# Rotary attention: the fourth turned fill of a pair moves from behind the first half of the values' projection to behind the third projection

## The reference, cut to what matters

```python
def _L0_attn_b_ref(x, Wq, Wk, Wv, Wo, bo):
    q = split_heads(x @ Wq); k = split_heads(x @ Wk); v = split_heads(x @ Wv)
    q = apply_rope(q); k = apply_rope(k)
    sim = jnp.einsum('bid,bjd->bij', q, k) * scale
    sim = jnp.where(causal[None], sim, -jnp.inf)
    attn = jax.nn.softmax(sim, axis=-1)
    out = jnp.einsum('bij,bjd->bid', attn, v)
    out = out.reshape(b, h, t, d).transpose(0, 2, 1, 3).reshape(b, t, h * d)
    return out @ Wo + bo
```

## Time and profile before

| | |
|---|---|
| median of the runs shown | 4107.78 us (4107.56 to 4110.89, 3 runs) |
| the profiled execution: its time | 4110.04 us |
| its span (first to last instruction) | 4108.3 us |
| the attention that the change touches | from about 1253 to 2720 us of the span |
| granted TensorE clock over the span | 0.911 |

### The profile page before, as it was taken

How to read it: one execution, slowest core, us unless ns; L and a number is a source line. 1 busy time by engine, 2 the same in 40 slices (tenths; PEclk the granted TensorE clock), 3 DMA queues, 4 the chain that set the end, 5 groups by cost and what they waited for, 6 DMA issues and landing times. The chain is left out here.

```text
span 4108.3 us, 88859 instructions
## 1 busy us (share of the span) xinstructions
PE 3521.3 (86%) x30527; PEld 2152.3 (52%) x30527; DVE 2730.1 (66%) x7270; ACT 2282.9 (56%) x5504; POOL 2039.0 (50%) x2055
## 2 busy tenths in 40 slices
PE   5999999967676999999999999985947776887768
PEld 1333333316673555655555555564936665675446
DVE  6888888856354777777777777754556664655465
ACT  2776777754233666666666666642435552674367
POOL 3333333217445676777767767656521111665175
PEclk9999999985797999999999999975979887898879
DMA  5434334302462121211212121122632221120001
GB/s 98 62 58 59 59 59 59 59 5 79 146 191 63 47 52 44 52 47 48 51 44 52 46 49 48 46 63 81 210 98 69 61 66 45 29 63 6 1 1 42
DMA packets 418239, 252.21 MB, mean 61 GB/s; under 512 B 251186, under 2 KB 344354, under 8 KB 416642
## 3 DMA queue, kind: packets, MB, share of 16 engines
q1 hardware_dynamic: 409156, 228.56, 24.2%
q0 software_dynamic: 8640, 17.97, 1.3%
HBM read 75.12 MB, written 41.75 MB: 28 GB/s over the span
## 5 line engine op out<-in xcount | busy, mean ns | idle before, releaser
L2499 POOL TENSOR_TENSOR ra_prob<-ra_prob,ra_inverse 128x256 f32<-128x256 f32 (+3 forms) x512 | 630.7, 1253 | 386.9 <-DVE ra_inverse L2715 386.6
L2313 DVE TENSOR_REDUCE ca_mx<-ca_ps_s 128x2 f32<-128x1024 f32 x512 | 601.0, 1211 | 122.5 <-PE ca_ps_s L2177 122.3
L2242 ACT ACTIVATE ca_pT<-ca_ps_p 128x512 f32<-128x512 f32 x1024 | 548.6, 602 | 219.6 <-PE ca_ps_p L2187 217.8
L2644 ACT ACTIVATE ra_prob<-ra_ps_s,ra_low 128x128 f32<-128x128 f32 (+3 forms) x1024 | 533.6, 531 | 237.8 <-DVE ra_low L2695 237.8
L2695 DVE CUSTOM_DVE_ANT_0 ra_ps_s<-ra_ps_s,ra_mask 128x128 f32<-128x128 f32 (+3 forms) x1024 | 475.3, 516 | 46.6 <-PE ra_ps_s L2592 46.4
L2177 PE MATMUL ca_ps_s<-ca_kst,ca_qst 128*128 128x512 bf16 x1024 | 394.5, 391 | 36.9 <-DVE ca_mx L2313 21.7
L2187 PE MATMUL ca_ps_p<-ca_qst,ca_kst 128*128 128x512 bf16 x1024 | 386.2, 382 | 4.4 <-ACT ca_pT L2242 3.9
L2650 ACT COPY ra_probT<-ra_ps_t 128x512 f32<-128x512 f32 x384 | 227.1, 591 | 278.6 <-PE ra_ps_t L2538 278.6
L2538 PE MATMUL ra_ps_t<-ident,ra_prob 128*128 128x128 f32 x2560 | 377.4, 278 | 5.1 <-POOL ra_prob L2499 1.2
L2538 PEld LDWEIGHTS ra_ps_t<-ident,ra_prob 128*128 128x128 f32 x2560 | 289.3, 141 | 124.2 <-issue 59.7
L2592 PE MATMUL ra_ps_s<-ra_kz,ra_qz 64*128 64x128 f32 (+3 forms) x2048 | 347.7, 458 | 3.7 <-DMA ra_kz<-ra_rot 2.8
(11 more groups left out here) (410 smaller groups left out, 7156.0 us busy)
## 6 DMA issues: line engine op xcount, KB each, us to landing
moe_w_own<-moe_w1T SPq DMA_DIRECT2D x142, 256.0 KB
ra_qz<-ra_rot SPq DMA_DIRECT2D x512, 64.0 KB, 2.0
ra_kz<-ra_rot SPq DMA_DIRECT2D x512, 64.0 KB, 2.0
ca_kst<-ca_bounce SPq DMA_DIRECT2D x256, 64.0 KB
ca_bounce<-ca_thirds SPq DMA_DIRECT2D x192, 64.0 KB, 2.8
ca_qst<-ca_bounce SPq DMA_DIRECT2D x64, 192.0 KB
moe_hs<-moe_rows SPq DMA_DIRECT2D x142, 66.0 KB
moe_raw<-in_L_ffn_W SPq DMA_DIRECT2D x32, 256.0 KB
```

Of the source, the lines that this page charges most:

```text
L2242: nc.scalar.activation(pT[:, (NS * hp + u) % PRING, :], ps_p[n % NP][:], ACT.Exp).then_inc(sg["drained"], 1)
L2313: nc.vector.tensor_reduce(mx[:, hm % 2, 2 * j:2 * j + 2], ps_s[m % 2][:].rearrange("p (b k) -> p b k", b=2), AX.X, ALU.max)\
L2499: nc.gpsimd.tensor_tensor(at, at, inverse[:, n % PROB, 2 * tile:2 * tile + 2].unsqueeze(2).broadcast_to([P, 2, keys]), ALU.mult)\
L2644: nc.scalar.activation(prob[:, n % PROB, tile, head, 0:keys], part(n, tile)[:, head, :], ACT.Exp, bias=low[:, n % PROB, at:at + 1], scale= ...
```

## The change

In the table of the turns, `turn(3)` leaves slot t=1 and goes to slot t=2, ahead of `turn(4)`. On TensorE it then stands behind `project(2)` or `project_out`, and no longer directly behind `turn(2)`. On DVE `fill(3)` moves with it, from ahead of the inverse of t=1 to behind `multiply(2)` or the addition to X, and ahead of `minima(2)`. No instruction is added or taken away, and the bank, the engine and the waits of each turn and fill stay as they are.

```diff
--- before.py
+++ after.py
@@ -2420,7 +2420,7 @@
         COPIES = 8
         landed = lambda n: 16 * COPIES * (n // RING + 1)
         VISITS = 3
-        fills = lambda t: ((0, 1), (2, 3), (4,), ())[t]
+        fills = lambda t: ((0, 1), (2,), (3, 4), ())[t]
         COPIED = (3, 2)
@@ -2726,8 +2726,10 @@
                     if score is not None and t == 0:
                         minima(0, score)
-                    if value is not None and t < 2:
-                        fill(2 * t + 1, value)
+                    if value is not None and t == 0:
+                        fill(1, value)
+                    if value is not None and t == 2:
+                        fill(3, value)
                     if t == 1 and 0 <= s - SCORE - 1 < PAIRS:
                         invert(s - SCORE - 1, 1)
```

## The result

| | before | after |
|---|---|---|
| median, both measured together (6 runs each) | 4107.67 us | 4141.03 us |
| lowest to highest | 4104.42 to 4111.05 | 4134.55 to 4148.47 |
| profiled execution, time (span) | 4110.04 (4108.3) us | 4135.67 (4134.0) us |

The changed kernel is slower by a ratio of 1.0081, 95% interval 1.0067 to 1.0095: 33 us of loss, 28 to 39. The forecast was 4143.5 us.

What follows compares the result with a forecast made beforehand. TensorE's instruction list was taken to bound the kernel (99.7% busy). 123 pairs x (0.53 new stop - 0.24 old stop) = 35.7 us on 4107.8 gave 4143.5 us, 4137 to 4147, widened to 4132 to 4160 for 8 in 10.

Steps and rivals of the forecast that it cites:

- The old stop, 0.24 us a pair: TensorE at turn(3), whose load waits for DVE's fill(1): 0.18 us waiting plus 0.06 restart, removed by the change.
- The new wait of 0.42 us behind the copy to v: TensorE, through with turn(2), waits 0.42 us before project(2) or project_out until ACT has copied v out of ps_r.
- The restart of 0.10 us: A projection starting without weights loaded ahead takes 0.10 us longer: L2563 1.12 for 1.02, L2573 2.05 for 1.95.
- The lower bound of 0.06: Restart of the projection bounded at 0.06 us, the transposes' price, giving a loss of 0.24 us a pair.
- The sum: Over the attention, 123 x (0.53 - 0.24) = 35.7 us more; bounds 29.5 and 39.4.
- The count of 123 pairs: Pair steps affected: 124 with a projection of v, less the first odd step, where nothing stands between the turns.
- It hangs on TensorE: ACT's copy to v would not come earlier against TensorE: a 2.61 us chain from turn(0) over fill(0) and exponentials.
- rival 1: Exponentials on ACT ahead of the copy to v start earlier, shrinking the new wait: faster, 4078.3 us; 7 in 100.
- fill(3) at no cost: On DVE, fill(3) pushes minima(2) by 0.32 us at most, covered by ACT's idle 0.73 and 1.88 us: cost nothing.
- rival 3: fill(3) ahead of minima(2) on DVE delays exponentials, fill(0) and the copy to v: slower still, 4168 us; 12 in 100.
- Rival 2: TensorE's pauses at changes between 64-row and 128-row matmuls shrink, up to 0.29 us: no change, 4108 us; 7 in 100.
- The two rules weighed: Skill's narrower weight-load rule: restart costs nothing, sum 29.5 us, 4137.3. Bank-rotation rule: speaks against the change, through the projections' single bank.

Runs made afterwards that it cites:

- early_narrow: Kernel before with fill(1) on DVE between the two heads' minima and ACT's copy to v cut to 32 of 512 columns: ratio 0.9925 to before.
- narrow_after: Changed kernel with ACT's copy to v cut from 512 to 32 columns from quad 3 on: ratio 0.9974 to the kernel before.
- narrow_before: Kernel before with ACT's copy to v cut from 512 to 32 columns from quad 3 on: ratio 0.9995 to the kernel before.
- vfirst_after: Changed kernel with ACT's copy to v ahead of the exponential of tile 1, head 0: ratio 1.0068 to the kernel before.
- dve_only: Kernel before with only DVE's half of the change, fill(3) moved and TensorE's order untouched: ratio 0.9997 to the kernel before.
- early_before: Kernel before with fill(1) on DVE between the minima of head 0 and head 1, TensorE's order untouched: ratio 0.9954 to before.
- early_vfirst: Kernel before with fill(1) between the two heads' minima and ACT's copy to v ahead of tile 1, head 0's exponential: ratio 0.9950.

## Why the prediction was right

**The old stop, 0.24 us a pair, removed.** Right. The waits behind L2709 went from 32.4 to 0.3 us, and early_narrow, which takes away both stops, gained 29.1 us in the steady part where 29.5 was the sum.

**The new wait of 0.42 us behind the copy to v.** Right: 0.43 in the even step shown, and 0.47 in the odd one (2021.71 - 2021.24). The copy still ends 0.37 us after the fourth transpose, as forecast. narrow_after and narrow_before show that it is this copy and nothing else.

**The restart of 0.10 us.** Right in size: 1.13 us for L2563 where 1.12 was taken, 2.02 for L2573 where the row had 2.05. L2573 also begins 0.10 us behind the copy's end and not 0.05, which more than makes up for the shorter row: the odd stop is 0.47 + 0.07 = 0.54 us, not 0.52. The lower bound of 0.06 wasn't needed.

**The sum.** 35.7 us against 36.9 in the steady part, 35.3 in the whole attention and 33 (28 to 39) in the times. The pair step from `turn(2)` to `turn(2)` was forecast at 11.44 us and took 11.45; the cost of a step is nearer 0.30 us than 0.29. The forecast lay 2.5 us over the median.

**The count of 123 pairs.** Right: the trace of after has 62 groups of `project(2)` and 61 of `project_out` directly behind `turn(2)`; 61 and 60 of their waits fall between 1300 and 2700 us.

**"It hangs on TensorE" - right, by a wrong step.** The prediction let the copy hang on a chain over `turn(0)`, `fill(0)` and two exponentials, 2.61 us, and made that chain's length the point from which rival 1 decides. vfirst_after took one exponential out of the chain and the copy moved by 0.03 us, because the end of `project(1)` was as late. Rival 1 as I gave it could never have come true by ACT's list alone: the copy can't start before its data. The row of L2554 that shows it (2013.28 and 1.03 us, ended 0.06 us ahead of the copy) was in the trace of before, and I didn't read it. Rival 1 was also priced too high: it gave the full 29.5 us for a copy 0.42 us sooner, and narrow_after, with the copy 0.40 us shorter, gained 11.4, because the restart stays until the load can start ahead.

**fill(3) at no cost.** Right: dve_only, and in the changed kernel ACT still idles 0.73 us (odd) and 1.87 us (even) ahead of `fill(0)`, as in the earlier trace rows, which is the sign that the prediction named for rival 3.

**The rivals.** Rival 2, pauses that shrink at L2592 and L2605, did not show. From 1300 to 2700 us, before and then after:

```profile
PEld ra_ps_o L2605 <- issue: 192.1, 692, 0.8
...
PEld ra_ps_s L2592 <- issue: 115.2, 251, 0.8
```

```profile
PEld ra_ps_o L2605 <- issue: 185.8, 671, 0.8
...
PEld ra_ps_s L2592 <- issue: 112.8, 244, 0.8
```

That is 0.28 and 0.46 us a pause in both; there are fewer because fewer pair steps fit into the stretch. The 1.12 us of the unmoved `project(0)` (2005.72 in after) is what the earlier trace rows has.

**The two rules weighed.** With a restart at nothing the sum was 29.5 us. The steady part's 36.9 and the first matmul's 697 ns for 595 speak for the overlap; the times alone (28 to 39) allow both. So the narrower rule on weight loads in the Trainium skill ("TensorE: Matmul & The Clock Gate", The mechanism) is not what this trace shows. The bank that doesn't rotate, `ps_r`, set the time. The rule on rotating banks in the Trainium skill ("Perfetto Trace Analysis", Optimizing Tensor Performance) pointed at that resource, and the trace agrees: narrow_after frees the bank earlier, and the loss is gone.

## What to carry to other kernels

A group that stands behind a stop may be the cover of another one. Before moving it, read when the next instruction in the list would be allowed to start: here 0.30 us of spare time under `turn(3)` turned into 0.43 of waiting. Where a consumer holds up a full TensorE, move the consumer on its own engine first: `fill(1)` between two minima on DVE gained 0.46% with TensorE's order untouched. And when one stop is taken out, the next wait in the list is met with that much less time, so its release and its weight load belong in the sum.

## What the runs showed of the hardware

A group of matmuls pays for a late release even where no wait is to be seen. In early_before the projection started the moment the last transpose was through, and took 1.12 us where a stream gives 1.02; with the bank free 0.03 us earlier it took 1.09, and with the copy out of the way it took 1.02 again and the whole 0.24 us of a pair came back. In the groups that paid nothing, the 128x128 fp32 load started 0.11 us before its matmul; no such group of any run has a lead between 0.04 and 0.10 us. Two of the ten expectations, narrow_after's and in part early_before's, missed by this, and early_vfirst's missed because the moved exponential cost the even steps what the lead gained.

The sixteen short matmuls of the output projection began 0.10 us behind the copy's end where `project(2)` began 0.05 to 0.06 behind it. Both lost some 0.17 us in all beyond the copy's end (0.10 + 2.02 - 1.95 and 0.06 + 1.13 - 1.02).
